# Attention and mixture-of-experts block on one core: projection before the convolution, its taps on ScalarE and VectorE, roots on ScalarE, scatters without a bounds check

## The reference

```
q, k, v = silu(causal_conv4(x @ W))          # per channel, 4 taps, for Wq, Wk, Wv
q, k    = q / |q|, k / |k|                   # per head, 4 heads of 32
beta    = sigmoid(x @ Wb);  Kb, Vb = k * beta, v * beta
A       = Kb @ k.T per chunk of 64 tokens;  T = (I + tril(A, -1)) ** -1
W, U    = T @ Kb, T @ Vb;  a scan over the 8 chunks carries a state S; its diagonal enters O
o       = O * rsqrt(mean(O * O) + 1e-5) * g;  x = layernorm(x + o @ Wo)
scores  = sigmoid(x @ gate_w.T); 4 of 8 groups, then 8 of 64 experts a token, weights normalised
x       = layernorm(x + sum over the chosen experts of w * mlp_e(x) + shared_mlp(x))
```

## Time and profile before

| | us |
|---|---|
| median of 3 runs | 1161.55 |
| lowest and highest run | 1159.23, 1168.6 |
| profiled execution, first to last instruction (span) | 868.7 |
| busy in the span: TensorE | 698.5 |
| busy in the span: VectorE | 489.8 |
| busy in the span: ScalarE | 322.0 |
| busy in the span: GpSimd | 548.9 |
| DMA queues, share of 16 engines: SyncE's, GpSimd's | 23.5%, 12.5% |

### The profile page before, as it was taken

How to read it: one execution, slowest core, us unless ns; L and a number is a source line. 1 busy time by engine, 2 the same in 40 slices (tenths; PEclk the granted TensorE clock), 3 DMA queues, 4 the chain that set the end, 5 groups by cost and what they waited for, 6 DMA issues and landing times.

```text
span 868.7 us, 17014 instructions
## 1 busy us (share of the span) xinstructions
PE 698.5 (80%) x4968; PEld 606.5 (70%) x4968; DVE 489.8 (56%) x1679; ACT 322.0 (37%) x867; POOL 548.9 (63%) x558
## 2 busy tenths in 40 slices
PE   5689797979888786767799998999897888961395
PEld 3567676767676666644587898988797887960385
DVE  2437878787777777755756663444334433430275
ACT  2224233333424242313043564664545536420032
POOL 0000277777777777676777777777777777777241
PEclk9898989897979796959579998999989989895599
DMA  8202041414141413111354444444434434311695
GB/s 199 77 1 89 15 140 59 144 62 142 59 142 60 137 52 107 51 61 47 98 149 123 118 122 126 117 108 130 115 102 127 110 100 115 104 41 51 263 408 215
DMA packets 89949, 97.47 MB, mean 112 GB/s; under 512 B 21836, under 2 KB 73780, under 8 KB 89859
## 3 DMA queue, kind: packets, MB, share of 16 engines
q1 hardware_dynamic: 67043, 58.45, 23.5%
q0 software_dynamic: 20992, 36.74, 12.5%
q10 hardware_dynamic: 1824, 1.19, 0.5%
HBM read 55.02 MB, written 42.34 MB: 112 GB/s over the span
## 4 chain that ended last, share of the span: by engine, by line
PE 38%; DVE 22%; issue 15%; POOL 12%; DMA 7%; SPq 2%; ACT 2%; POOLq 0%; ACTq 0%; DVEq 0%
POOL y_dram L463 12%; DMA y_dram<-arena 4%; PE fa L1215 3%; PE fc L1140 3%; PE pb L1165 3%; PE pa L1165 2%; PE fb L1140 2%; PE ba L1145 2%; DMA arena<-y_dram 2%; DVE arena L720 2%; PE fa L1145 2%; PE bb L1140 1%; PE bb L1361 1%; PE ba L1361 1%; PE fb L1382 1%
## 5 line engine op out<-in xcount | busy, mean ns | idle before, releaser
L463 POOL DMA_INDIRECT y_dram<-arena x272 | 266.4, 979 | 83.4 <-issue 73.8
L444 POOL DMA_INDIRECT rows_dram<-rows x256 | 256.9, 1004 | 97.6 <-issue 76.4
L435 POOL TENSOR_TENSOR rstd<-var_eps,minus_half 128x2 f32<-128x2 f32 (+1 forms) x24 | 25.3, 1055 | 132.6 <-DVE var_eps L662 132.6
L618 ACT ACTIVATE arena<-weights 128x176 f32 x384 | 99.0, 337 | 13.8 <-DVE arena L1025 13.2
L1079 DVE TENSOR_TENSOR arena<-bb,arena 128x512 f32<-128x512 f32 x34 | 23.5, 691 | 75.5 <-DMA y_dram<-arena 70.9
L1140 PE MATMUL fb<-arena 128*128 128x128 f32 x384 | 53.7, 284 | 14.6 <-DVE arena L720 14.0
L1140 PEld LDWEIGHTS fb<-arena 128*128 128x128 f32 x384 | 48.8, 195 | 20.9 <-DVE arena L720 13.5
L1079 DVE TENSOR_TENSOR arena<-ba,arena 128x512 f32<-128x512 f32 x34 | 23.5, 690 | 67.1 <-DMA y_dram<-arena 63.3
L1140 PEld LDWEIGHTS fc<-arena 128*128 128x128 f32 x384 | 50.0, 197 | 15.2 <-ACT arena L522 7.7
L607 ACT ACTIVATE arena<-fb 88x512 f32<-88x512 f32 x39 | 23.1, 592 | 99.3 <-PE fc L1382 89.2
L1361 PE MATMUL bb<-weights,arena 88*128 x336 | 47.9, 293 | 14.4 <-DVE arena L1113 13.8
(11 more groups left out here) (295 smaller groups left out, 1472.6 us busy)
## 6 DMA issues: line engine op xcount, KB each, us to landing
arena<-y_dram SPq DMA_DIRECT2D x16, 1024.0 KB, 12.1
arena<-rows_dram SPq DMA_DIRECT2D x192, 76.0 KB
weights<-experts SPq DMA_DIRECT2D x16, 608.0 KB
arena<-rows_dram SPq DMA_DIRECT2D x128, 38.0 KB
y_dram<-arena POOLq DMA_INDIRECT x272
rows_dram<-rows POOLq DMA_INDIRECT x256, 2.3
xc<-x_chan SPq DMA_DIRECT2D x8, 256.0 KB, 3.9
x_res<-x_tok SPq DMA_DIRECT2D x8, 256.0 KB, 3.0
```

Of the source, the lines that this page charges most:

```text
L435: pool.tensor_tensor(rstd[b % 2][:, 0:tiles], var_eps[b % 2][:, 0:tiles], minus_half[:, 0:tiles], ALU.pow).then_inc(S.rstd_done, 1)
L444: pool.indirect_dma_start(rows_dram, bass.IndirectOffsetOnAxis(ap=slot_of(a)[:, i, k:k + 1], axis=0), rows[:, NT * a + i, :], None).then_i ...
L463: pool.indirect_dma_start(y_dram, bass.IndirectOffsetOnAxis(ap=go_to[:, t:t + 1], axis=0), y_sb[q % YRING][:, i, :], None, bounds_check=B ...
L618: ins = act.activation(w_here[n % 2][:, (parts(q) * i + h) * 2 * I:(parts(q) * i + h + 1) * 2 * I], weights[:, bass.ds(at[i], 2 * I)], ACT ...
```

## The change

- **Projection first.** For each of k, v and q one matmul over 512 columns gives the projection with channels on partitions (`y`); four small ones give beta (`bt`). ScalarE copies the projection out of PSUM, scaled by the last tap (`c`), and VectorE adds the other three taps, each a fused multiply and add over shifted columns that reads the projection in PSUM (`d1` to `d3`). TensorE turns the result back to tokens first (`t`), and SiLU follows, for each of k, v and q. The tap matrices, their loads and the padding of `xc` go.
- **Roots.** Both Newton iterations, and the power on GpSimd in the first part, become a square root on ScalarE (`hrt`, `rrt`, `std`) and a reciprocal on VectorE (`hrn`, `rrn`, `rstd`). In the second part `rstd` stays on GpSimd.
- **The inverse.** The transposed inverse of level 0 is no longer a predicated copy on VectorE with masks of its own, but a transpose on TensorE (`invt0`) and a copy on ScalarE (`cpt0`). Half of the masks go. k and kb are turned into other PSUM banks (`fc`, `fa`).
- **Order.** All positions are new: a block's steps span 148 to 677, where they spanned 14 to 391, with `CYCLE` still at 145. GpSimd sends the scatters block after block. The small preparations (`prep`: bias, `wo_g`, a bf16 copy, `carry`) become VectorE's first step in the walk and wait for all small loads, `places` now among them.
- **Scatters of the second part.** No bounds check. Filling rows go to distinct rows of a sink of 2048 rows at the front of `y_dram`. The destination is the maximum of the row's place and its sink row.
- **Loads.** x, Wk and the small tap weights come first; constants are loaded in two pieces; most loads are on SyncE's queue. A few semaphores are merged.

The diff, cut to its core:

```diff
-NOWHERE = 1 << 20
+RING, YRING, W_RING = 4, 4, 6
+SINK = 4 * YRING * P
...
+AT = dict(prep=10, yk=147.942, ck=152.685, dk1=161.773, dk2=196.976, bt=203.048, siluk=224.373, tk=234.876,
+          tb=235.032, sqk=242.6, dk3=243.648, yv=246.078, cv=247.565, cq=249.438, yq=252.214, hrtk=260.791,
+          sumk=263.751, dv1=265.713, dv2=265.833, dq1=268.249, dv3=270.303, hrnk=274.879, dq2=276.784, dq3=276.967,
+          tv=278.58, normk=280.231, siluv=281.239, tq=286.482, kb=293.647, siluq=297.041, sqq=299.949, hrtq=311.715,
+          sumq=313.156, hrnq=322.909, vb=338.671, kt_c=340.371, normq=343.469, kt=346.011, kbt_c=348.645, eye=361.573,
+          nat=362.463, kbt=363.784, at=372.498, aa=374.595, invt0=384.221, z1=384.958, cpt0=385.396, zc1=388.849,
+          inv1=400.106, z2=400.24, cp0=400.527, dot=403.124, invt1=403.334, cp1=410.626, zc2=416.815, inv2=418.818,
+          cpt1=419.689, cp2=420.39, invt2=426.977, z3=427.474, cpt2=439.518, zc3=439.625, inv3=440.164, cpt3=445.252,
+          zc4=445.767, cp3=445.769, invt3=446.516, z4=449.344, cp4=464.733, cpt4=465.53, inv4=466.226, zc5=467.85,
+          invt4=468.433, z5=468.726, inv5=477.429, xk=486.038, cp5=487.209, g=490.504, spread=492.062, p1=495.75,
+          cs=508.181, p2=510.336, ts=516.003, scan=518.66, tr=528.551, y1=534.647, osd=540.657, t1=541.468,
+          osq=544.455, u=549.831, res=550.327, o=550.795, rms=559.12, rrn=562.8, rrt=565.161, on=579.432, to=586.369,
+          to_c=588.883, wo=596.868, mom=604.212, std=606.058, x1=610.096, rstd=615.484, x1t=621.017, x1t_c=621.875,
+          logits=623.44, tanh=625.002, shift=625.819, r0=634.319, sc=637.358, r1=637.697, r2=647.85, rank=656.518,
+          r3=658.868, r4=669.336, r5=669.509, r6=672.605, r7=672.941, r8=674.556, key0=676.079, key1=676.152,
+          key2=676.939)
...
             pool.memset(minus_half[:, :], -0.5)
-            pool.memset(half[:, :], 0.5).then_inc(S.half_set, 1)
-            pool.wait_ge(S.places_in, 16)
-            pool.wait_ge(S.half_set, 1)
-            for _, a, n in sorted([(a * CYCLE + AT["rstd"], a, -1) for a in range(B)]
-                                  + [(a * CYCLE + at, a, n) for a in range(B) for n, at in enumerate(SPREAD)]):
-                if n < 0:
-                    inverse_std(a)
-                else:
+            pool.memset(ln_eps[:, :], LN_EPS)
+            pool.memset(rms_eps[:, :], RMS_EPS)
+            pool.memset(half[:, :], 0.5).then_inc(S.pool_set, 1)
+            pool.wait_ge(S.small_in, 16 * 10)
+            pool.wait_ge(S.pool_set, 1)
+            for a in range(B):
+                for n in range(NT * TOPK):
                     scatter(a, n)
...
                     pool.indirect_dma_start(y_dram, bass.IndirectOffsetOnAxis(ap=go_to[:, t:t + 1], axis=0),
-                                            y_sb[q % YRING][:, i, :], None, bounds_check=B * L * PLACES - 1,
-                                            oob_is_err=False).then_inc(ys[q % YRING], 16)
+                                            y_sb[q % YRING][:, i, :], None).then_inc(ys[q % YRING], 16)
...
+                for j, m in enumerate(KVQ):
+                    if op == f"c{m}":
+                        act.wait_ge(S.y_mm, 3 * a + j + 1)
+                        if a >= 1:
+                            act.wait_ge(S.turn_mm, 3 * (a - 1) + j + 1)
+                        act.activation(conv[j], y_bank(m)[:, :], ACT.Copy,
+                                       scale=conv_w[:, j, KS - 1:KS]).then_inc(S.tap0_done, 1)
+                    if op == f"silu{m}":
+                        act.wait_ge(S.turn_mm, 3 * a + j + 1)
+                        if a >= 2:
                             act.wait_ge(S.dot_done, a - 1)
                             act.wait_ge(S.osd_done, a - 1)
+                        act.activation(qkv[n][:, :, COLS[m]], by_tile(y_bank(m)[:, :]), ACT.Silu).then_inc(S.qkv_act, 1)
...
+                    if op == f"hrt{m}":
+                        act.wait_ge(S.ss_done, 2 * a + j + 1)
+                        if a >= 1:
+                            act.wait_ge(S.hrn_done, 2 * (a - 1) + j + 1)
+                        act.activation(head_rt[:, 16 * j:16 * (j + 1)], head_ss[:, 16 * j:16 * (j + 1)],
...
+                    if op == f"cpt{k}":
+                        act.wait_ge(S.invt_mm, (LEVELS - 1) * a + k + 1)
+                        if k == 0 and a >= 2:
+                            act.wait_ge(S.tr_mm, a - 1)
+                        act.activation(inv_t[n], fa[:, :], ACT.Copy).then_inc(S.invt_done, 1)
...
+                if op == "rrt":
+                    act.wait_ge(S.t_done, a + 1)
+                    if a >= 1:
+                        act.wait_ge(S.rrn_done, a)
+                    act.activation(rms_rt[:, :], rms_ss[:, :], ACT.Sqrt, bias=rms_eps[:, 0:1],
+                                   scale=1.0 / HD).then_inc(S.rrt_done, 1)
+                if op == "std":
+                    act.wait_ge(S.mv_done, a + 1)
+                    if a >= 2:
+                        act.wait_ge(S.rs_done, a - 1)
+                    act.activation(std[n][:, :], mean_var[n][:, :, 1], ACT.Sqrt, bias=ln_eps[:, 0:1]).then_inc(S.std_done, 1)
...
+                for j, m in enumerate(KVQ):
+                    done = (S.conv_k, S.conv_v, S.conv_q)[j]
+                    for k in range(1, KS):
+                        if op == f"d{m}{k}":
+                            if k == 1:
+                                dve.wait_ge(S.tap0_done, 3 * a + j + 1)
+                            else:
+                                dve.wait_ge(done, (KS - 1) * a + k - 1)
+                            dve.scalar_tensor_tensor(out=conv[j][:, k:L], in0=y_bank(m)[:, 0:L - k],
+                                                     scalar=conv_w[:, j, KS - 1 - k:KS - k], in1=conv[j][:, k:L],
+                                                     op0=ALU.mult, op1=ALU.add).then_inc(done, 1)
...
+                    if op == f"hrn{m}":
+                        dve.wait_ge(S.hrt_done, 2 * a + j + 1)
+                        if a >= 1:
+                            dve.wait_ge(S.qk_done, 2 * (a - 1) + j + 1)
...
+                if op == "prep" and a == 0:
+                    dve.wait_ge(S.small_in, 16 * 10)
+                    dve.wait_ge(S.consts_in, 32)
+                    dve.tensor_scalar(bias_b[:, :], bias_b[:, :], 0.5, None, ALU.add).then_inc(S.prep_done, 1)
+                    dve.tensor_scalar(wo_g[:, :], wo_g[:, :], g_col[:, 0:1], None, ALU.mult).then_inc(S.prep_done, 1)
+                    dve.tensor_copy(tri_b[:, :], const[:, K_TRI:K_TRI + P]).then_inc(S.prep_done, 1)
+                    dve.tensor_copy(carry[0][:, :], const[:, K_BASE:K_BASE + E]).then_inc(S.carry_done, 1)
...
-                    dve.tensor_scalar(go_to[:, 4 * q:4 * q + 4], w_at[q % W_RING][:, :, 1], float(NOWHERE), None, ALU.add).then_inc(S.go_done, 1)
+                    dve.tensor_tensor(go_to[:, 4 * q:4 * q + 4], w_at[q % W_RING][:, :, 1],
+                                      const[:, K_SINK + 4 * (q % YRING):K_SINK + 4 * (q % YRING) + 4], ALU.max).then_inc(S.go_done, 1)
...
-                    if op not in (f"proj{i}a", f"proj{i}b"):
-                        continue
-                    ps = (pa, pb)[i % 2]
-                    if op == f"proj{i}a":
+                for j, m in enumerate(KVQ):
+                    if op == f"y{m}":
                         pe.wait_ge(xc_in[n], 16 * (a // 2 + 1))
-                        if i < 2 and a >= 1:
-                            pe.wait_ge((S.kt_done, S.kbt_done)[i], a)
-                        if i >= 2:
-                            pe.wait_ge(S.qkv_act, NT * a + i - 1)
-                    for k in (3, 2) if op == f"proj{i}a" else (1, 0):
-                        if i < 2 and a == 0:
-                            pe.wait_ge(S.tap_made, KS - k)
-                        m = QKVB if k == KS - 1 else QKV
-                        at = i * P + k + 1
-                        mm = pe.matmul(ps[:, 0:m], xc[n][:, at:at + P], tap[:, k, 0:m], start=(k == KS - 1), stop=(k == 0))
-                    if op == f"proj{i}b":
-                        mm.then_inc(S.qkv_mm, 1)
+                        if a == 0:
+                            pe.wait_ge((S.wk_in, S.wvq_in, S.wvq_in)[j], (16, 64, 64)[j])
+                        if bank_free(a, m) > 0:
+                            pe.wait_ge(S.qkv_act, bank_free(a, m))
+                        pe.matmul(y_bank(m)[:, :], w_qkv[:, COLS[m]], xc[n][:, :], start=True, stop=True).then_inc(S.y_mm, 1)
+                    if op == f"t{m}":
+                        if a == 0:
+                            pe.wait_ge(S.wvq_in, 64)
+                        pe.wait_ge((S.conv_k, S.conv_v, S.conv_q)[j], (KS - 1) * (a + 1))
+                        turned(y_bank(m), lambda i: blk(conv[j], i)).then_inc(S.turn_mm, 1)
+                if op == "bt":
+                    pe.wait_ge(xc_in[n], 16 * (a // 2 + 1))
+                    if a == 0:
```

(28 more changed lines are left out.)

316 lines of the change are left out of this document (138 added, 178 removed).

## The result

The changed kernel took 1236.03 us (median of four runs, 1230.81 to 1238.75) and kernel before 1160.39 (1156.73 to 1168.60) on the same chip. The ratio is 1.0621, 95% interval 1.057 to 1.0672: 6% slower, where 1138 us and a gain were forecast.

A forecast was written before the change was run, and what follows sets the result against it. GpSimd's scatter issue was taken as the bound, nearly even with compute in the first part. First y scatter -19.0, bounds check -5.2, tail and surroundings 0: 1161.55 - 24.2 = 1137.4, stated as 1138 us, range 1114 to 1168.

The forecast's parts named there:

- 292.9 us lie outside the span: Around the kernel: median 1161.55 us minus profiled span 868.7 us, taken as surroundings that the change leaves alone.
- T: First part, time per block between consecutive blocks' first scatters: 42.3 us forecast, from 44.5 in steady blocks before.
- first scatter: GpSimd's first row scatter, block 0: forecast at 103 us, between 98 and 112, where it was at 102.77.
- first y scatter: Start of the second part: forecast at 440.6 us instead of 459.6, a gain of 19.0 us.
- unchecked scatters: Second part: 272 y scatters without bounds check, each 1.267 instead of 1.286 us, 5.2 us less.
- nearly even match: First part of kernel before: GpSimd's scatters, stretching, rstd and its wait were taken to fill blocks about as compute does.
- four table loads per block: ScalarE, first part: changes between SiLU or tanh and square root, 1.28 us each, 5.1 us per block.
- Rival A: First part: square-root loads and waits on ScalarE delay the inversion's copies, 47.4 us per block, 1178 us; chance 0.14.
- C: Rival: GpSimd is the wall from start to end, first scatter at 98 us, total 1123 us; chance 0.16.
- D: Rival: dropping the y scatters' check saves nothing, forecast plus 5, 1143 us; counted within the forecast's chance of 0.52.
- B: Rival: VectorE's new tap work replaces what it loses, blocks stay at 44.5 us, total 1153 us; chance 0.18.
- a gain of some 3 us per block: GpSimd, first part: it loses the rstd operation, 1.08 us, and its wait, 1.97 us for block 1.

The follow-up runs named there:

- chip of 1160: One of two kinds of chips met in the runs: the unchanged kernel before takes 1161 to 1196 us on five of these.
- chip of 870: The other kind of chip met in the runs: the unchanged kernel before takes 869 to 870 us on four of these.
- the version with three waits: Changed kernel, GpSimd waiting before a block's 9th, 17th and 25th row scatters for inversion copies two blocks ahead: 851.88 us (0.980) and 1153.25 us (0.9919).

## Why the prediction was wrong

**The step that failed is the first: "292.9 us lie outside the span" and "I carry that sum over unchanged".** They lay inside the time, between the first row scatter and the last y scatter. On the chip of 1160 with a trace of kernel before these two parts take 514.3 and 506.3 us, where the earlier trace rows has 356.8 and 349.9: 157 and 156 us more. In the first part that is compute that nearly stands while GpSimd scatters; in the second the trace looks the same, and no run tests it. The profile of before is one of a chip of 870, the times are of chips of 1160. Everything behind it was worked out for a condition that the measured runs did not have. The term was the difference of a row and a median that did not belong together, and nothing in the trace stood for it. What followed from it is that T, forecast at 42.3 us per block, was 75.0, and the y scatters, forecast 1.267 us apart, 1.82.

**On a chip of 870 the rest held**, term by term:

| term | forecast | measured |
|---|---|---|
| first tap | 14.5 | 13.6 |
| first scatter | 103 (98 to 112) | 110.6 |
| T, by the first scatters of blocks 0 to 7 | 42.3 | 41.6 |
| TensorE, VectorE, ScalarE busy per block | 32.9, 35.4, 22.2 | 31.9, 34.3, 24.6 |
| first y scatter | 440.6 | 442.0 |
| unchecked scatters | -5.2 | -6.6, in kernel before (870.46 to 863.85) |
| tail | 59.2 | 59.5 |
| span | 844.5 | 848.5 |

The busy times are a third of each in this row, three blocks of the changed kernel on a chip of 870:

```profile
193.29:317.50 124.21, 95.57 (x664) 79.61 (x662) 102.98 (x333) 73.76 (x126) 94.23 (x95) 0.92 0.31 103
```

Part of this is luck. The first scatter was 7.6 us later than forecast, inside its bounds, and T, 0.7 us shorter seven times, gave 5 of them back. And two readings were off. In kernel before GpSimd was called the other side of a nearly even match and its wait a part of its need; compute alone takes 44.6 us there, some 1.3 more than GpSimd's own stream. On ScalarE the prediction counted four table loads per block, and there are five: after the root of `std` the router's tanh loads a table, and the next SiLU loads another, though kernel before has one load for both functions. That is 1.3 of the 2.4 us by which ScalarE was over its forecast.

**Rival A** (the roots stall the inversion) gave a time on the right side for a wrong reason. The roots stay in the version with three waits, and it is 0.8% below kernel before. The one root that was moved by itself into the old order, with about two table loads per block, costs 1.5 to 1.8% on chips of 870, which fits A's mechanism at a small size. **C** had GpSimd as the wall from an early first scatter on. On a chip of 870 its 328 us from there to the first y scatter are near the 331.4 measured, but that scatter came at 110.6 and not at 98; on a chip of 1160 GpSimd waits 34 us per block. **D** was wrong: without the check the y scatters take 5 us less. **B** holds on neither kind of chip.

**What the change did on a chip of 1160** is a thing that no rival named: it took the rstd out of the stream of scatters, and with it the pause of 7.7 to 15.1 us in which compute caught up. The prediction costed the loss of that pause as a gain of some 3 us per block. Putting a pause back took the changed kernel from 1.062 to 1.017, three waits alone to 0.992, and taking it out of kernel before, with the root moved to ScalarE, cost 4.9%. From the two traces, before (1184.80 us) and after (1235.06): first row scatter 103.1 to 109.7, +7; from there to the first y scatter 514.3 to 569.3, +55; y scatters and the last of them 506.3 to 495.0, -11; tail the same, 59. That is +50. The recorded medians are 76 apart; the other 25 us lie in kernel before, which was at 1160 on the recorded chip and at 1185 to 1196 on the one of this trace, and no trace of before exists on the recorded one. The changed kernel was not run on that slower chip, so the parts of the +50 are of two chips and understate what the change costs on one.

Not settled: how scatters hold the compute engines on these chips, and what the chips differ in. The traces show releases that come late and from an unknown place, and compute that goes on at about 60% of its records for some 15 us before it nearly stands. The scatters themselves take 0.96 us on both kinds, and the packets of GpSimd's queue take the same time: 9.0% of 1233.2 us and 13.1% of 848.5 us, 111 us of the 16 DMA engines either way.

## What to carry to other kernels

Compare the span on the page with the timed runs before anything else: here a gap of a quarter of the time was not surroundings but another condition, and the first experiment should be the unchanged kernel. A wait on an engine that sends indirect DMAs can be worth keeping: where these hold up compute, one long stream costs more than the same scatters with pauses, and a semaphore wait on a step that is normally early is a pause that cost nothing measurable here where it wasn't needed (0.980 with it, 0.976 without). And a bound that is inferred from a near-even sum should be tested by taking one side away (held scatters, one run) before it carries a forecast.

## What the runs showed of the hardware

On chips of 1160 a block takes 41.3 us without row scatters and 75.0 with 32 of them in a row, and the y scatters come 1.82 us apart instead of 1.27, while each scatter's own duration is unchanged (0.96 us). The granted clock of the stand is low, 0.57 of full speed over 273.5 to 299.0 us, where the same stretch on a chip of 870 has 0.87. The slow-down comes first: over 184.0 to 199.0 us the clock is 1.00 and TensorE has 50 records, where the same 15 us of a block have 82 on a chip of 870. The clock falls after that, and in block 2's 35 us without scatters it is still at 0.72.

A table load came straight behind the activation before it (116.20 + 0.64 = 116.84, the load at 116.85), took 1.28 us, and the root started 0.02 us after it. The Trainium skill, "ScalarE: Activation LUTs", What ACT_TABLE_LOAD costs, gives 2.66 us for a switch with a drain of 1.38; this trace, on a busy engine, has the load and no drain, and the measurement decides.
